# Cross attention takes head groups 0 and 1 before 2 and 3, with other steady order strings

## What is computed

```
x = layernorm(x + self_attn(x))            # 16 heads of 8, keys = queries = x, full softmax,
                                           # weight (16*128, 128)
x = layernorm(x + cross_attn(x, ctx))      # 16 heads of 8, Wq Wk Wv Wo with biases,
                                           # scores masked to |i - j| <= 64
y = x
for l in 0, 1:                             # 8 heads of 64
    q, k, v = split(shift(y) @ wqkv[l]); q, k = rotary(l2norm(q)*qs, l2norm(k)*ks)
    y = y + softmax(window(q k^T)) v @ wo[l]
    h = layernorm(shift(y)) ; a, g = split(h @ w1[l] + b1[l])
    y = y + (a * gelu(g)) @ w2[l] + b2[l]
x = layernorm(x + y)
```

## Time and profile before

| what | value |
|---|---|
| median of 3 runs | 1372.78 us |
| the profiled execution's own time | 1370.2 us |
| span of its trace | 1368.4 us |
| mean granted TensorE clock | 0.980 |
| VectorE (DVE) busy | 1068.8 us, 78% of the span |
| ScalarE (ACT) busy | 978.5 us, 72% |
| GpSimd (POOL) busy | 760.4 us, 56% |
| DMA | 9 GB/s over the span |

### The profile page before, as it was taken

How to read it: one execution, slowest core, us unless ns; L and a number is a source line. 1 busy time by engine, 2 the same in 40 slices (tenths; PEclk the granted TensorE clock), 3 DMA queues, 4 the chain that set the end, 5 groups by cost and what they waited for, 6 DMA issues and landing times. The chain is left out here.

```text
span 1368.4 us, 41673 instructions
## 1 busy us (share of the span) xinstructions
PE 1293.9 (95%) x13496; PEld 907.8 (66%) x13496; DVE 1068.8 (78%) x3190; ACT 978.5 (72%) x2688; POOL 760.4 (56%) x843
## 2 busy tenths in 40 slices
PE   4999999999999999999999999999999999999874
PEld 2566666777766677776667777666777766676653
DVE  3667888888888888888888888888888888888652
ACT  2357777777787777778777777877777787777763
POOL 1135665555666555566655556665555666555642
PEclk9799999999999999999999999999999999999986
DMA  5000000000000000000000000000000000000000
GB/s 167 11 6 2 6 8 7 6 2 6 6 6 4 6 6 2 6 6 6 4 6 6 2 6 6 6 4 6 6 2 6 6 6 4 6 5 4 4 1 6
DMA packets 21042, 12.44 MB, mean 9 GB/s; under 512 B 4700, under 2 KB 19846, under 8 KB 20998
## 3 DMA queue, kind: packets, MB, share of 16 engines
q1 hardware_dynamic: 18790, 8.04, 2.1%
q10 hardware_dynamic: 2208, 3.84, 0.8%
HBM read 9.78 MB, written 2.10 MB: 9 GB/s over the span
## 5 line engine op out<-in xcount | busy, mean ns | idle before, releaser
L1276 POOL TENSOR_TENSOR local_rn<-local_sc,half_neg 128x8 f32<-128x8 f32 x128 | 210.8, 1647 | 69.5 <-DVE local_sc L1127 69.5
L1297 POOL TENSOR_TENSOR local_e<-local_e,local_rd 128x512 f32<-128x512 f32 x128 | 133.0, 1039 | 197.5 <-DVE local_rd L1144 197.5
L938 ACT ACTIVATE local_e<-local_ps,local_bias,local_rn 128x128 f32<-128x128 f32 x512 | 228.9, 467 | 13.5 <-DVE local_bias L1140 13.4
L665 PE MATMUL self_ps<-self_z,self_e 128*128 128x129 f32 x1024 | 146.1, 285 | 2.5 <-ACT self_e L865 1.3
L687 PE MATMUL local_ps<-wz,self_kT 128*128 128x512 f32 x256 | 138.0, 624 | 5.7 <-ACT self_kT L871 5.6
L1059 DVE SCALAR_TENSOR_TENSOR self_y<-self_ps,self_rd,self_y 128x128 f32<-128x128 f32 x448 | 133.0, 344 | 9.5
L665 PEld LDWEIGHTS self_ps<-self_z,self_e 128*128 128x128 f32 x1024 | 127.4, 193 | 11.7 <-DVE self_y L1059 2.3
L1280 POOL TENSOR_TENSOR local_cosp<-local_cosp,local_sinp 128x512 f32<-128x512 f32 x64 | 81.2, 1269 | 86.7 <-DVE local_sinp L1119 86.6
L1135 DVE TENSOR_REDUCE local_m<-local_ps 128x4 f32<-128x512 f32 x128 | 87.9, 686 | 39.3 <-PE local_ps L586 38.6
L918 ACT ACTIVATE local_sq<-local_ps 128x512 f32<-128x512 f32 x128 | 75.9, 593 | 47.7 <-PE local_ps L747 43.1
L938 ACT ACTIVATION_READ_ACCUMULATOR local_e<-local_ps,local_bias,local_rn 128x1 f32 x512 | 109.6, 214 | 0.0
(11 more groups left out here) (175 smaller groups left out, 3312.5 us busy)
## 6 DMA issues: line engine op xcount, KB each, us to landing
self_xin<-x SPq DMA_DIRECT2D x32, 64.0 KB, 1.8
cross_cin<-ctx_in SPq DMA_DIRECT2D x32, 64.0 KB, 1.8
out<-local_out SPq DMA_DIRECT2D x32, 64.0 KB, 1.6
wqkv_s<-wqkv ACTq DMA_DIRECT2D x2, 768.0 KB, 9.7
wz<-w_heads ACTq DMA_DIRECT2D x4, 256.0 KB, 5.9
w_r<-w ACTq DMA_DIRECT2D x2, 341.0 KB, 11.5
con<-consts SPq DMA_DIRECT2D x1, 640.0 KB, 6.6
wo_s<-wo ACTq DMA_DIRECT2D x2, 256.0 KB, 10.8
```

What stands on the lines that cost most here:

```text
L665: last = nc.tensor.matmul(bank[:, 129 * j:129 * j + 129], s.e[:, h0 + j, :], s.z[:, h0 + j, :], start=True, stop=True)
L938: nc.scalar.activation(s.e[:, a, p, :], bank[:, 128 * p:128 * p + 128], ACT.Exp, bias=s.bias[:, a, p:p + 1], scale=s.rq[:, a, p:p + 1], ac ...
L1276: nc.gpsimd.tensor_tensor(s.rn[:, heads], s.sc[:, heads], half_neg[:, 0:LH], ALU.pow).then_inc(done, STEP)
L1297: nc.gpsimd.tensor_tensor(s.e[:, a, :, :], s.e[:, a, :, :], s.rd[:, a, :].unsqueeze(2).to_broadcast([128, LH // 2, 128]), ALU.mult)\
```

## The change

`CROSS.pairs` becomes ((0, 1), (2, 3)), in all phases. The warm-up and cool-down strings stay. The steady strings of four engines change in the order of steps, and the DMA string too. No instruction is added or removed.

```diff
@@ ORDER_TENSOR, steady
-    ("ONAOAONABPSPBABPZSCZBSACAZSDSCSDCZSSCCBBSSCEECCCSDDSSDCCCSDEEMCCECME"),
+    ("ONAOAONABPSPPBABPZSCZBSACAZSDCSSDCZSSCCBBSSCEECCCSDDSSDCCCSDEEMCCECME"),
@@ ORDER_VECTOR, steady
-    ("NNNONOAAAAPABBPSSBPSSCCCABBDCDCBCDCSDSDESEDSESSESSPSESESSDSMSMMCCSMCOCEC"),
+    ("NNNONOAAAAAPABPBSSBSSCCCBBDCDCDPCDOCBSSDEDESSSSEEPSESSESSSDSMMSMCCMSCCEC"),
@@ ORDER_SCALAR, steady
-    ("KOAANBAPSBASYBZCZBAASCZSSZDSSBBDCDDEEDDCCEEDCCEEEM"),
+    ("KOAANBASPBSABYZCZBAACZSSSZDSSBBDCDDEEDDCCEEDCCEEEM"),
@@ ORDER_GPSIMD, steady
-    ("ONBSANASABAAPBABBBDDEECSMMC"),
+    ("NNBSSAAAAABBABBPBODDEECSMMC"),
 ORDER_SYNC = (
-    "CSP")
+    "CPS")
@@ SELF.windowed, CROSS.windowed = False, True
-        SELF.pairs, CROSS.pairs = ((0, 1), (2, 3)), ((2, 3), (0, 1))
+        SELF.pairs, CROSS.pairs = ((0, 1), (2, 3)), ((0, 1), (2, 3))
```

More of the change, by code:

```diff
@@ L76 @@
      "SDSCEEMCECME"),
-    ("ONAOAONABPSPBABPZSCZBSACAZSDSCSDCZSSCCBBSSCEECCCSDDSSDCCCSDEEMCCECME"),
+    ("ONAOAONABSPPBABPZSCZBSACAZSDCSSDCZSSCCBBSSCEECCCSDDSSDCCCSDEEMCCECME"),
     ("ONAOAONASPBPABSBPZZSCBACSZSSCCAZSCSCDDBCBSSCCEECSDCCCDSSCCDECSEDEMAEAMNOOAAONBPPBBPAACBCDCDCBBCCECECCCDCCCDCCD"
```

## The result

The changed kernel takes 1385.28 us (median of 4 runs, 1379.52 to 1385.42). The kernel before, on the same chip, takes 1374.01 (4 runs, 1372.36 to 1375.51). The ratio is 1.008, with a 95% interval from 1.0059 to 1.0101. So it is slower, by more than the 0.3% that can be told from no change, and by more than three times the forecast.

The account below looks back on a forecast made before the run. TensorE, busy 95%, was taken as the bound, through its order of starts. 0.07 us per iteration times 26 (1.8) plus 1.5 gave 3.3 us slower, 1376.1 us; own range 1373.8 to 1378.3, with rivals 1367 to 1383.

Parts of the forecast that it names:

- VectorE late in the iteration: Steady loop: later sum of squares, so D's weights are scaled about a microsecond later; charged 0.03 us, bounds 0 and 0.25.
- rival 3: The late scaling of D holds TensorE's transposes, up to 0.25 us per iteration, 6.5 us more, 1382 us; chance 0.12.
- Z4 and S7: Two successive TensorE steps, 1.06 us apart: an earlier VectorE reduction was to save 0.08 us, bounds 0 and 0.11.
- C3: bf16 products on TensorE, now ahead of a float32 set on the same rows: costs 0.22 us, bounds 0.01 and 0.33.
- C5: TensorE step held by the second cross maximum, behind D's GpSimd-blocked bias: 0.10 us gained, bounds 0 and 0.11.
- Rival 1: The exposure stays: C5 still follows the maximum, 0.25 us lost per iteration, 1380.8 us; chance 0.22.
- The turn of the loop: Between iterations: the wait of L818 goes but is waited for again; zero, bounds 0 and 0.23 + 0.15 us.
- rival 2: The loop's turn shortens by 0.38 us per iteration, net 6.6 us faster, 1366.2 us; chance 0.16.
- S1, S3, GpSimd's S2, DMA order: Reordered steps on TensorE, ScalarE and GpSimd and reordered loads: hidden or not waited for, each forecast at zero.
- Warm-up and cool-down: Phases outside the steady loop: new pairs put some sets on equal rows; 1.5 us slower, bounds 0 and 3.

Follow-up runs that it names:

- second set: The changed kernel run again with no edit, against the kernel before: 1379.79 us (6 runs), ratio 1.0062.

## Why the prediction was wrong

The direction was right, the size was not: 11.3 us between the medians where 3.3 were forecast. Point by point.

**VectorE late in the iteration: the step that failed.** The prediction said that the scaling of D's weights comes a microsecond later and that "E's first bias may also meet a GpSimd instruction", and charged 0.03 us for these ties. They measured 0.21, 5.5 us over the loop. The mechanism was named but not followed. The bias feeds four exponentials, these and the copy L949 fill ScalarE without a gap, and TensorE's D6 comes 0.21 us behind that copy already before the change. I had looked at the second scaling and TensorE's transposes (rival 3), which don't wait. Its upper bound of 0.25 happened to hold the price, which was luck: it was put on a place that doesn't wait. The order of the events would have been readable: in the trace of before the scaling ends 0.42 us ahead of the bias, and a scaling a microsecond later covers it.

**Z4 and S7.** The forecast gain of 0.08 didn't come. B5 ends 1.4 us before Z4 in the new trace, and the distance is 1.06 as ever:

```profile
637.74 0.68 DVE L1119 TENSOR_TENSOR local_sinp<-local_ps,sin_t 128x512 f32<-128x512 f32 x1
```

So the reading of the earlier trace rows was wrong: the late B5 wasn't what made 1.06 of 0.95. What differs between the two places is what stands in front of Z4: in the steady part the mask of C3 (L576, a matmul of 64 rows and 64 columns), in the cool-down transposes that use the full array. The trace of before holds more such places. From the first product of an L687 set to its second it is 0.43 us behind products that use 113 or 128 rows (L837, L702 and L767, 26 times each), and 0.53 behind the mask of 64 rows (26 times) and behind products of 32 rows (L595 and L614, once each in the warm-up); two sets that start 0.05 us behind the transpose L636 have 0.49. So 0.10 of the 0.11 goes with the smaller tile in front. This is read from places of one trace; no experiment took the mask away. The Trainium skill, "TensorEngine Tiling (Array Packing)", section "Key Properties", says that a change of the tiling mode drains the engine, and that different tiles can load weights and multiply in parallel. The 0.53 against 0.43 agrees, and so do C3 and S5 on different rows (0.02 us).

**C3.** Forecast 0.22; S5 alone follows C3 by 0.233, and the stretch from D1 to S6 is 0.187 longer, as S6 follows S5 by 0.05 less. Right.

**C5.** Forecast -0.10; measured -0.105, and 0.007 at C6 and 0.029 at C7 on top. The size was right and the cause half right. It is the bias that was held by GpSimd, as the prediction read from two ends 0.02 us apart. The same ends coincide in the changed kernel (607.65 and 607.64), with the pairs alone (639.46 and 639.44), with the strings alone and with VectorE's order of before on old pairs, be it D's bias or E's, and it takes 0.41, 0.34, 0.19, 0.35 and 0.30 us in these five, by how much of GpSimd's instruction is left when it starts. The Trainium skill, "SBUF — State Buffer", section "SBUF: two separate sides", calls the shared port pair an exclusive lock that the first comer keeps for its whole instruction; the traces agree, with a bias of 0.13 to 0.16 us that takes up to 0.41 when it comes second. But the new string of VectorE wasn't needed for this gain: it also comes with the pairs alone and with the old string. Rival 1, that the exposure stays, fell.

**The turn of the loop.** Forecast zero; 1.841 and 1.842 us. The wait of L818 went and the time was waited for in the next steps, so rival 2 fell.

**S1, S3, GpSimd's S2, DMA order.** Forecast zero, and no distance there moved.

**Warm-up and cool-down.** Forecast 1.5 us. The traces have +1.0 and +0.9, but the two profiled executions of the changed kernel differ there by 5.1 and 3.0 us, so this term can't be checked by totals and stays open. Single places can. C5's and C3's sets behind S6 cost 0.22 us on equal rows and 0.02 on different ones in the warm-up after, as forecast. S5 and C8, now on the same rows, run one behind the other (43.66 and 44.62), and S7 follows S5 by 3.44 us instead of 2.92: 0.52 where 0.4 was forecast.

**The sum.** The terms but D6 were forecast at 0.22 - 0.08 - 0.10 = 0.04 and measured at 0.187 - 0.112 - 0.029 = 0.046. That these agree is partly luck, as the gain of 0.08 at Z4 that didn't come is made up by the 0.187 for 0.22, by C6 and by C7. The error of the loop is D6: 26 x (0.21 - 0.03) = 4.7 us. The other 3.3 of the 8.0 us lie outside the loop, where 1.5 was forecast for 4.8 between the medians. The times of both kernels fall in two groups some 5 us apart: before, 1372.4 and 1372.8 against 1375.2 and 1375.5; changed, 1379.5 against three times 1385.3 to 1385.4. The median of the changed kernel's first set is in its upper group, and the one of before lies between its groups. Lowest with lowest the difference is 7.2 us, highest with highest 9.9, between the profiled executions 9.3, and 7.75 between the medians of the second set. The range ended at 1383, 2.3 us too low for the first set. It allowed a loss in the loop of 0.25 us per iteration, which was about right, and had no room for this spread between executions. What the spread consists of is in the last section.

## What to carry to other kernels

When a step is moved to a later place, follow it through each queue that it feeds, up to the next step of the bounding engine, even if that is three engines and 9 us away: here VectorE, GpSimd, VectorE again by the shared port, ScalarE, TensorE. Look for short VectorE instructions with two SBUF inputs whose consumers wait, and see which GpSimd instruction will be running when they are due; put them ahead of anything that only feeds a slack engine. A pair of changes searched together should be taken apart on the chip: here the pairs cost 0.08 us per iteration alone and 0.13 to 0.16 on top of the new strings, VectorE's string cost about 0.2, and the rest of the strings gave 0.09, or 0.26 with B6, D's second bias and E's first bias moved on VectorE.

## What the runs showed that was not expected

A producer that is in time by 0.05 us is late all the same. From D6's first product to its second it is 0.213 us in the three programs in which the copy ends 0.05 us ahead of D6, 0.138 in the two in which it ends 0.13 ahead, and 0.111 in the five in which it ends 0.21 ahead (D6 to E3 0.995, 0.920 and 0.892). In the changed kernel none of the loss at D6 stands in the list of waits.

The matmuls of the first microseconds run at one of two speeds, and not the same in each execution. These are TensorE's rows for the same two matmuls and four later ones, first in the kernel before, then in the second set of the changed kernel; the code up to there is the same.

```profile
15.75 1.12 PE L687 MATMUL local_ps<-wz,self_kT 128*128 128x512 f32 x2
...
18.00 1.13 PE L608 MATMUL self_ps<-self_qm,self_kT 32*128 32x512 f32 x4 [0.43 <-ACT self_negT L859]
```
```profile
15.97 2.08 PE L687 MATMUL local_ps<-wz,self_kT 128*128 128x512 f32 x2
...
18.58 2.08 PE L608 MATMUL self_ps<-self_qm,self_kT 32*128 32x512 f32 x4 [0.43 <-ACT self_negT L859]
```

The durations of 1.12 and 2.08 us fit the two levels of 2.4 and 1.2 GHz. TensorE's rows start at the same times in both up to 15.43 us, and the two matmuls of L687 from 13.42 on take 2.08 us in both. The granted clock of the windows from 15 to 25 us is 1.00 in both traces, but that isn't a reading: the trace's records of the granted clock begin at 15.4 us in the first and at 30.2 in the second, each time with the upper level, and a stretch without a record is counted as 1.00. The matmuls agree with the records. In the second trace those of L665 take 0.42 us each up to 30.0 and 0.27 to 0.28 from 30.2 on. What decides when TensorE rises is open.

This is most of the spread outside the loop. Between the two profiled executions of the changed kernel the late rise costs 5.1 us by 36.8 us from the start. The warm-up takes 170.5 to 173.7 us in seven of the eleven profiled executions and 177.2 to 178.0 in four. These four have their first record between 28.9 and 30.4 us. They have the new pairs, as two of the seven do. The kernel with the strings alone also rises late, at 29.6, and has 173.7; its granted clock from 90 to 105 us is 1.00, where the second set of the changed kernel has 0.90. Whether the pairs make the late rise more frequent is open. The cool-down goes with the clock too: from 1285 to 1320 us the granted clock of the changed kernel is 0.89 and 0.88 in the first profile and 1.00 in the second, whose cool-down is 3.0 us shorter.

```profile
1300.00:1320.00 20.00, 15.67 (x91) 9.69 (x83) 13.36 (x34) 12.12 (x29) 14.35 (x15) 0.88 0.00 1
```
```profile
1300.00:1320.00 20.00, 15.76 (x120) 10.08 (x120) 14.15 (x40) 12.08 (x27) 15.19 (x17) 1.00 0.01 4
```

The columns are the stretch, its length, the busy time of TensorE, its weight loads, VectorE, ScalarE and GpSimd, the granted clock, and the DMA's share and GB/s. No trace was kept of the three executions near 1385.3, so that they are of the late kind is not shown. For a measurement this means that 5 us of such a kernel's time are outside the change that is studied, that the mean granted clock doesn't show the late rise, and that the period of the loop in a trace tells more than a median of a few runs.
